# Half of the final sums moved from VectorE to TensorE, in the last stage of a fused graph and expert network

## What is computed

```python
x = x + gat(layernorm(x), adj)           # graph attention
x = x + moe0(layernorm(x))               # 8 experts, top 2
x = x + gated_graph(layernorm(x), adj)   # three message passing layers with a GRU
x = x + moe1(layernorm(x))               # 16 experts, top 2
```

## Time and profile before

| | us |
|---|---|
| median of 3 runs | 1059.63 (1057.14 to 1060.46) |
| the profiled execution | 1060.54 |
| its span, first to last instruction | 1058.6 |
| TensorE busy | 949.2 (90%) |
| VectorE busy | 765.4 (72%) |
| ScalarE busy | 554.1 (52%) |
| GpSimd busy | 590.6 (56%) |

### The profile page before, as it was taken

The page is one execution under the profiler, slowest core; times in us unless marked ns, Lnnn a source line. Parts: engine busy times, 40 slices in busy tenths (PEclk is TensorE's granted clock), DMA queues, the critical chain, the costliest instruction groups (busy, mean ns, idle before and its releaser), DMA issues. The chain is left out here.

```text
span 1058.6 us, 24167 instructions
## 1 busy us (share of the span) xinstructions
PE 949.2 (90%) x6368; PEld 769.4 (73%) x6369; DVE 765.4 (72%) x2973; ACT 554.1 (52%) x1358; POOL 590.6 (56%) x623
## 2 busy tenths in 40 slices
PE   4776999999999997799999999999956899999970
PEld 3665999999989997455555555655536899999970
DVE  5557888888876666378898989989775555555558
ACT  4654665565553342355566655766533344444455
POOL 2155777777777755001356445564536777766670
PEclk9558999999999999799999999999986999999995
DMA  9611422222222422211303223040013543333349
GB/s 225 226 38 61 102 79 81 77 79 73 81 84 74 118 72 86 81 40 41 95 26 103 63 66 105 26 135 26 31 35 82 127 127 95 90 91 90 90 168 364
DMA packets 101512, 99.36 MB, mean 94 GB/s; under 512 B 32412, under 2 KB 86300, under 8 KB 101148
## 3 DMA queue, kind: packets, MB, share of 16 engines
q1 hardware_dynamic: 84252, 62.83, 21.4%
q0 software_dynamic: 17152, 35.29, 9.9%
HBM read 55.44 MB, written 42.62 MB: 93 GB/s over the span
## 5 line engine op out<-in xcount | busy, mean ns | idle before, releaser
L440 POOL DMA_INDIRECT queue<-rows,slots x256 | 259.0, 1012 | 161.5 <-issue 68.8
L2261 POOL DMA_INDIRECT result<-y_rows,y_ids x144 | 144.2, 1001 | 56.9 <-issue 48.3
L1026 POOL DMA_INDIRECT result<-y_rows,y_ids x136 | 134.8, 991 | 61.4 <-issue 35.7
L2292 PE MATMUL e_ps_h<-e_xT,e_up_of 128*128 128x128 f32 x1152 | 143.2, 278 | 2.7 <-DVE e_hT L2405 2.7
L2292 PEld LDWEIGHTS e_ps_h<-e_xT,e_up_of 128*128 128x128 f32 x1152 | 136.8, 195 | 3.5 <-issue 2.9
L1573 PEld LDWEIGHTS a_ps_y<-w_sb,a_hT 128*128 128x128 f32 x1088 | 131.1, 192 | 4.1 <-issue 1.3
L1573 PE MATMUL a_ps_y<-w_sb,a_hT 128*128 x1088 | 132.6, 275 | 1.1 <-DVE y_rows L1185 1.1
L1557 PE MATMUL a_ps_up<-a_xT,a_up_of 128*128 128x256 f32 x448 | 106.9, 381 | 1.1 <-DVE a_up_of L1156 0.8
L2405 DVE TENSOR_TENSOR e_hT<-e_ps_h,e_gate 128x512 f32<-128x512 f32 x72 | 49.7, 690 | 72.6 <-ACT e_gate L2340 70.9
L2340 ACT ACTIVATE e_gate<-e_ps_h 128x512 f32<-128x512 f32 x72 | 43.0, 597 | 96.8 <-PE e_ps_h L2292 95.5
L1557 PEld LDWEIGHTS a_ps_up<-a_xT,a_up_of 128*128 128x128 f32 x448 | 80.7, 190 | 11.8 <-issue 1.5
(11 more groups left out here) (287 smaller groups left out, 2071.4 us busy)
## 6 DMA issues: line engine op xcount, KB each, us to landing
xq<-queue SPq DMA_DIRECT2D x168, 64.5 KB
g_y<-result SPq DMA_DIRECT2D x20, 512.0 KB, 4.3
xq<-queue SPq DMA_DIRECT2D x56, 129.0 KB
result<-y_rows,y_ids POOLq DMA_INDIRECT x280, 2.3
x_res<-x SPq DMA_DIRECT2D x16, 256.0 KB, 3.9
w_sb<-w SPq DMA_DIRECT2D x2, 2048.0 KB, 12.0
queue<-rows,slots POOLq DMA_INDIRECT x256, 2.4
w_sb<-w SPq DMA_DIRECT2D x16, 256.0 KB, 4.0
```

The costliest lines, as they stand in the source:

```text
L440: pool.indirect_dma_start(out=queue, out_offset=bass.IndirectOffsetOnAxis(ap=c.slots[q][:, k, t:t + 1], axis=0), in_=c.rows[q][:, k, t, :] ...
L1026: pool.indirect_dma_start(out=c.result0, out_offset=bass.IndirectOffsetOnAxis(ap=ids[slot.k][:, t, :].bitcast(U32), axis=0), in_=y[slot.k] ...
L2261: pool.indirect_dma_start(out=result, out_offset=bass.IndirectOffsetOnAxis(ap=ids[at_down.k][:, t, :].bitcast(U32), axis=0), in_=y[at_down ...
L2292: last = pe.matmul(ps_h[b][:, t, q * P:(q + 1) * P], up_of[at_up.k % 4][:, t, q * P:(q + 1) * P], xT[at_up.k % 4][:, t, :], start=True, st ...
```

## The change

In the odd groups VectorE's additions are split otherwise. ScalarE still scales `y1`. TensorE then makes two products with the identity matrix into one PSUM bank of `ps_h`: the first brings `p1 * y1` of the four tiles (512 columns), the second adds the residual `x` of the same tiles. It raises `mixed`. VectorE waits for `mixed` and does four instructions of 128x128 that add `p0 * y0` to the PSUM sum and write the result into the residual; the addition of 128x512 is gone in these groups. The four banks of `ps_h` are used in turn, one for each odd group; from the fifth odd group on TensorE waits for `added` of the group that used the bank before. The even groups stay as they were, with `first_added` counted by even groups now. SP and ScalarE are unchanged.

```diff
@@ experts, set-up
+        banks = [ps_h[b][:, t, :] for b in range(2) for t in range(PAIR)]
@@ experts, TensorE's program
             steps(pe, body, 0, 4)
+            finish.mix(pe, banks)
@@ experts, VectorE's program
                 steps(v, gated_body, 2, 4, between)
-                finish.sum(v)
+                finish.sum(v, banks)
@@ class Finish
+    def mix(self, pe, banks):
+        c = self.c
+        for s in range(1, NG, 2):
+            y, bank = self.y[s % OUT_BUFFERS], banks[s // 2 % len(banks)]
+            if s // 2 >= len(banks):
+                pe.wait_ge(self.added, s - 2 * len(banks) + 1)
+            pe.wait_ge(self.scaled, s + 1)
+            pe.matmul(bank, c.ident[:], y[:, :, 1, :], start=True, stop=False)
+            pe.matmul(bank, c.ident[:], c.x[:, s * G:(s + 1) * G, :], start=False, stop=True).then_inc(self.mixed, 1)
+
-    def sum(self, v):
+    def sum(self, v, banks):
         c = self.c
         for s in range(NG):
-            y = self.y[s % OUT_BUFFERS]
+            y, bank = self.y[s % OUT_BUFFERS], banks[s // 2 % len(banks)]
             v.wait_ge(self.arrived[s % OUT_BUFFERS], (s // OUT_BUFFERS + 1) * 16)
-            for t in range(G):
-                last = combine(v, c, y, t, 0, s)
-            last.then_inc(self.first_added, 1)
-            v.wait_ge(self.first_added, s + 1)
-            v.wait_ge(self.scaled, s + 1)
-            xs = c.x[:, s * G:(s + 1) * G, :]
-            v.tensor_tensor(xs, y[:, :, 1, :], xs, ALU.add).then_inc(self.added, 1)
+            if s % 2:
+                v.wait_ge(self.mixed, s // 2 + 1)
+                for t in range(G):
+                    tile = s * G + t
+                    last = v.scalar_tensor_tensor(out=c.x[:, tile, :], in0=y[:, t, 0, :], scalar=c.prob[:, 0, tile:tile + 1],
+                                                  in1=bank[:, t * D:(t + 1) * D], op0=ALU.mult, op1=ALU.add)
+                last.then_inc(self.added, 1)
+            else:
+                for t in range(G):
+                    last = combine(v, c, y, t, 0, s)
+                last.then_inc(self.first_added, 1)
+                v.wait_ge(self.first_added, s // 2 + 1)
+                v.wait_ge(self.scaled, s + 1)
+                xs = c.x[:, s * G:(s + 1) * G, :]
+                v.tensor_tensor(xs, y[:, :, 1, :], xs, ALU.add).then_inc(self.added, 1)
```

## The result

The changed kernel takes 1062.89 us (median of 16 runs), the kernel before 1060.38 us in the runs beside them: a ratio of 1.0026 with a 95% interval of 1.0017 to 1.0035, or +2.8 us (1.8 to 3.7); the two medians alone are 2.5 us apart. That is within the 0.3% that the prediction called "same", on the slower side, and the interval doesn't reach a ratio of 1: the change costs a little. The profiled execution took 1063.92 us. The page of the changed kernel: its span, and the slices of VectorE and of DMA, in tenths.

What follows compares the result with a forecast made beforehand. The prediction took the transfers, not VectorE, to bound the final stage. The last group's +1.93 us at full clock less 0.3 us of queueing gave +1.6 on the median 1059.63: 1061.2 us, range 1058.2 to 1064.0.

Steps and rivals of the forecast that it cites:

- same: Whole kernel: a measured time between 1056.4 and 1062.8 us, not told from no change; chance 0.73.
- a clock near 0.5 in the last group: TensorE in group 15: a granted clock of 0.5 would show the prediction wrong; 1.0 was expected at 1053 to 1055.
- a last store that landed in under 2.8 us: End of the store queue: the last store landing in under 2.8 us would show the prediction wrong.
- The transfers set the pace, VectorE's 4.6 us are worth nothing.: Final stage: loads arrive 2.01 us apart, so 4.6 us saved on VectorE in eight odd groups doesn't show at the end.
- The last group has no cover: +1.93 us at the high clock, +3.68 at the low.: Group 15: the last add comes 1.93 us later at full clock, 3.68 at half, before 0.3 us less for queueing.
- full clock: TensorE's products in the last group run at 2.4 GHz: +1.6 us net; chance 0.52.
- half clock: Rival: TensorE's products in the last group run at 1.2 GHz: +3.4 us, 1063.0 us; chance 0.27.
- An idle stretch of 1.9 us keeps the clock high.: TensorE between odd groups: idling 1.9 of 4.0 us, shorter than the 2.2 before an earlier fall, leaves the clock high.
- The last store pays at most 0.3 us of queueing.: End of the store queue: of the last store's 3.3 us at most 0.3 is queueing, against 3.0 unloaded.
- The late load 9 costs nothing.: Stage start: store 1 and load 9 are issued up to 3.7 us late, priced at nothing, up to 1.7 if uncovered.
- A PSUM operand costs nothing.: VectorE's four instructions in odd groups: the PSUM operand adds nothing, with 0.2 us as the upper end.
- The loads' own time stays.: Loads of the final stage: the last one still lands at about 1052.1 us after a like span start.

Runs made afterwards that it cites:

- group 15 alone: The kernel before with only group 15 sent to TensorE and all other groups left as they were; ratio to the kernel before 1.0034.
- group 1 stays: The changed kernel with group 1 left to VectorE, the odd groups 3 to 15 on TensorE; ratio to the kernel before 1.0038.
- the four profiles: Changed kernel, its rebuild with ineffective empty instructions, one leaving group 1 to VectorE, one with 64 early small products; tail plus close 8.39, 8.32, 7.40, 7.48 us.

## Why the prediction was right, and where its steps were off

The prediction put the kernel in "same" and gave 1061.2 us with a range of 1058.2 to 1064.0; 1062.89 is in it. The mechanism was right, the place in the range in part luck. Two of the signs that the prediction itself had named as wrong appeared in the profile: a clock near 0.5 in the last group, and a last store that landed in under 2.8 us. The last addition ended at 1059.34 and not near 1056.6.

- *The transfers set the pace, VectorE's 4.6 us are worth nothing.* Right, and shown: without 9 us of VectorE's work the ratio is 1.0001.
- *The last group has no cover: +1.93 us at the high clock, +3.68 at the low.* Right, in size too. With both products at the low clock (group 15 alone) the tail grew by 3.70, with both at the high one (group 1 stays) by 1.96. In the changed kernel's profile it grew by 2.89, between the two values: the clock fell amid the products. The prediction set full clock, 0.52, against half clock, 0.27; the profiles have the first and a mixture. What it left out is that a wait in group 13 reaches the last group too: without group 15 on TensorE the tail was still 4.14.
- *An idle stretch of 1.9 us keeps the clock high.* Half right. It held over six groups, one of them begun after 2.22 us without work, and then fell 0.9 us into a group begun after 2.05. The 2.2 us after which it had fallen before divides nothing: the length of the idle stretch alone doesn't tell whether the clock stays. The Trainium skill's account (TensorE: Matmul & The Clock Gate, "HAM oscillation") is of bursts that are shorter than the wait for a transfer between them and start cold each time. By the prediction's own figures, 2.1 us of work against 1.9 of idling, it didn't apply, and the measured 1.95 against 2.05 hardly test it: of seven bursts after the first none began cold, and one didn't stay at the high level.
- *The last store pays at most 0.3 us of queueing.* This was the mis-sized term: 0.3 forecast, 1.0 measured. It was taken from a load of the same size, 3.0 us; the last store of the changed kernel, with no backlog left, landed in 2.3, and the close fell by 1.02. It is the part of the tail that the queue of stores hides, and it makes 6.5 us the least for tail and close together.
- *The late load 9 costs nothing.* Right. Store 1 went out at 1034.09 (forecast 1033.6), VectorE waited 4.05 us, and leaving group 1 alone gave nothing back.
- *A PSUM operand costs nothing.* Right: four instructions took 1.12 us with PSUM against 1.13 without, 1.29 only the first time. The 0.26 us worked out in the prediction from the Trainium skill (VectorE: DVE Perf Modes, the TRN2 errata) didn't show.
- *The loads' own time stays.* Wrong by 0.65 us. No step of the sum had a term for it, and its cause stays open: it comes with the longer program of TensorE and its fetch, but the fetch wasn't shown to be what does it. The Trainium skill (Runtime: NRT & Kernel Launch, "Instruction fetch mechanics") calls the cost of crossing a 16 KiB boundary mostly hidden; if the fetch is the cause, it wasn't hidden here, where all 16 engines were full of loads.

Put together with the measured sizes: loads +0.65, tail +2.9, close -1.0 gives +2.5 us for the changed kernel with the clock falling in the last group, against 2.8 measured (1.8 to 3.7). With the mean of the four profiles' tail and close, 7.90, it is +2.0, in the interval as well. The forecast of +1.6 had two errors of opposite sign in it, -0.7 for the queue and +0.65 for the loads, which nearly cancel; the rest is the clock. That they cancel is luck. The 1061.2 us lie 1.7 below the measured median; 0.75 of that is that the kernel before also reads 1060.38 in the larger set of runs.

No version of these beats the kernel before. The one without VectorE's additions shows why: what sets the length of the stage is 12.6 MB of transfers and the drain of stores, and relieving VectorE of more work than the change does gave nothing.

## What to carry to other kernels

An engine that is 98% busy needn't be the bound: look whether its producer waits for transfers, and whether its backlog grows or shrinks. Work moved to an idle engine makes the last item's chain longer by that engine's latency, and in a stage that the transfers pace it counts only for the last items and for those whose delay isn't made up before the end; put the new step ahead of the wait that it doesn't need. A backlog of stores hides a late last item up to a measurable amount, here 1.0 us.

## What was not expected of the hardware

- A slightly longer program of TensorE brought on a fetch of 16 KB of instructions that took about 1.0 us of one DMA engine, and in the profiles with it the last load landed 0.65 us later on average; that one causes the other isn't shown. The fetch appeared 7 us after the first load's issue also where the added instructions had been done for 2 us.
- With some 2 us of work in every 4, TensorE's clock fell once in each of four profiles, in the last group in two and in group 9 in two, each time with TensorE at work. In the last group it then took 3.1 us from scaled to VectorE's start instead of 2.2.
- VectorE's and the stores' shares of the last 6.5 us trade against each other to 0.04 us, in profiles of different kernels and in those of the same kernel.
